# A graph network layer on one core: TensorE subtracts h in the node update, x+h becomes one operation, one row of four is normalised on VectorE, and the edge update is rectified in transposed form

## What is computed

```python
h = jnp.maximum(_layernorm(x, axis=-1), 0.0)
em = jnp.concatenate([h[src], h[dst]], axis=-1)
em = jax.nn.relu(layer_norm(em @ msg_w + msg_b, msg_g, msg_beta)) * edge_weights[:, None]
msgs = jax.ops.segment_sum(em, dst, num_segments=num_nodes)
messages = msgs / (counts + 1e-08) * valid
gate = jax.nn.sigmoid(h @ gate_w + gate_b)
combined = jnp.concatenate([h, messages], axis=-1)
h_new = jax.nn.relu(layer_norm(combined @ upd_w + upd_b, upd_g, upd_beta))
out = x + gate * h_new + (1.0 - gate) * h
```

## Time and profile before

| | |
|---|---|
| three runs, median | 1056.28 us (1055.12 to 1071.27) |
| the profiled execution | 1053.59 us |
| its span, first to last instruction | 1052.1 us |
| DVE, ACT, PE, POOL busy | 79%, 77%, 69%, 58% of the span |
| mean granted TensorE clock | 0.834 |

### The profile page before, as it was taken

One profiled execution on the slowest core, in us unless ns is written; L12 is line 12 of the kernel. 1 busy time (PEld: TensorE's weight loads), 2 busy tenths in 40 slices (PEclk: granted clock), 3 DMA queues, 4 the chain that ended last, 5 costly groups with the idle time before them and its releaser, 6 DMA issues.

```text
span 1052.1 us, 20637 instructions
## 1 busy us (share of the span) xinstructions
PE 729.7 (69%) x4448; PEld 588.4 (56%) x4448; DVE 833.7 (79%) x3740; ACT 811.5 (77%) x3396; POOL 605.7 (58%) x602
## 2 busy tenths in 40 slices
PE   2377686776767677777666547777777778778772
PEld 2256565654545556555545336666665667667661
DVE  7287888886877888778789347999999988888984
ACT  2378787877868788778779258999999977878973
POOL 5555555554545555555555746666666666665557
PEclk9787978887888887788776668999989888988986
DMA  5255655565655666566532211322221121111110
GB/s 147 76 177 175 209 182 190 187 200 179 196 173 192 215 198 199 171 200 206 192 117 68 90 38 62 95 92 83 94 89 54 62 70 54 61 63 58 65 67 34
DMA packets 74548, 133.66 MB, mean 127 GB/s; under 512 B 16134, under 2 KB 18006, under 8 KB 74482
## 3 DMA queue, kind: packets, MB, share of 16 engines
q1 hardware_dynamic: 53868, 97.58, 27.1%
q0 software_dynamic: 18912, 34.84, 11.8%
q10 hardware_dynamic: 1702, 0.53, 0.2%
HBM read 56.01 MB, written 80.81 MB: 130 GB/s over the span
## 4 chain that ended last, share of the span: by engine, by line
ACT 47%; PE 16%; another core or an unknown queue 15%; issue 11%; DVE 7%; POOL 3%; ACTq 1%; DMA 0%; DVEq 0%; POOLq 0%; SPq 0%
ACT hrow L406 14%; ACT junk L413 13%; ACT xload L406 4%; ACT work L444 3%; PE py L1290 3%; POOL out L626 3%; PE pt L1248 3%; ACT lnv L388 2%; PE pm L1313 2%; ACT work L1159 2%; PE pm L1315 2%; ACT rs L393 2%; ACT at L1099 1%; PE py L1254 1%
## 5 line engine op out<-in xcount | busy, mean ns | idle before, releaser
L626 POOL DMA_INDIRECT out<-work,sidx x196 | 202.7, 1034 | 135.3 <-issue 54.2
L413 ACT ACTIVATE junk<-py 128x128 bf16<-128x128 f32 x588 | 155.7, 292 | 74.8 <-remote 64.2
L621 POOL DMA_INDIRECT ring<-in_x,gidx x140 | 141.9, 1013 | 89.7 <-DVE work L465 47.4
L406 ACT ACTIVATE hrow<-xload,nb,rs 128x128 f32<-128x128 f32 x392 | 163.9, 525 | 1.6 <-issue 0.8
L621 POOL DMA_INDIRECT ring<-in_x,src_i x116 | 116.3, 1002 | 68.4 <-issue 31.5
L1290 PE MATMUL py<-w_u,work 128*128 128x129 f32 x784 | 144.9, 341 | 0.0
L1290 PEld LDWEIGHTS py<-w_u,work 128*128 128x128 f32 x784 | 122.7, 238 | 28.2 <-issue 28.2
L413 ACT ACTIVATION_READ_ACCUMULATOR junk<-py 128x1 f32 x588 | 130.7, 223 | 0.0
L1254 PE MATMUL py<-bias,ones 3*128 3x258 bf16 x294 | 66.8, 313 | 77.6 <-ACT work L1099 56.8
L621 POOL DMA_INDIRECT work<-in_x,gidx x56 | 55.8, 996 | 108.9 <-DVE work L465 97.9
L1248 PE MATMUL pm<-ident,work 128*128 128x128 f32 x376 | 72.4, 325 | 63.4 <-ACT work L1104 31.9
(11 more groups left out here) (179 smaller groups left out, 2049.0 us busy)
## 6 DMA issues: line engine op xcount, KB each, us to landing
xload<-in_x SPq DMA_DIRECT2D x98, 256.0 KB
normalised_rows<-hrow SPq DMA_DIRECT2D x98, 256.0 KB
out<-work SPq DMA_DIRECT2D x98, 256.0 KB
running_sums<-acc SPq DMA_DIRECT2D x49, 256.0 KB
staged_target_rows<-work SPq DMA_DIRECT2D x14, 256.0 KB
ring<-staged_target_rows SPq DMA_DIRECT2D x14, 256.0 KB, 2.8
out<-work,sidx POOLq DMA_INDIRECT x196
ring<-in_x,gidx POOLq DMA_INDIRECT x140
```

The costliest lines, as they stand in the source:

```text
L406: last = nc.scalar.activation(dest[:, m, :], rows[:, m, :], ACT.Relu, bias=nb[:, s4, at + m:at + m + 1], scale=rs[:, s4, at + m:at + m + 1])
L413: last = nc.scalar.activation(junk[:, j, k, :], prod[:, k, 0:H], ACT.Square, scale=scale, accum_out=mv[:, slot, at + k, 1:2])
L621: pool.indirect_dma_start(out=dest, out_offset=None, in_=rows, in_offset=bass.IndirectOffsetOnAxis(ap=idx, axis=0), **({} if rows is sums_ ...
L626: pool.indirect_dma_start(out=out, out_offset=bass.IndirectOffsetOnAxis(ap=idx, axis=0), in_=rows, in_offset=None, **if_tail).then_inc(s, 16)
```

## The change

It has four parts, and constants that go with them.

1. **PE subtracts h.** `out = x + h + gate * (rectified - h)`, which is the same sum. In the node stage PE follows the four transposes back with four products of the transposed h and a negative identity into the same accumulation (`back`). Then x + h needs no gate: DVE makes it in one instruction of 512 columns for a group, in place of four of 128 columns, and 1 - gate isn't made there.
2. **One row of four normalised on VectorE.** ACT normalises rows 0 to 2 of a group in the node stage. Row 3 (`LIFTED`) is `(x - mean) * deviation` in one DVE instruction, `lifted_row`, not rectified. The copy out of PSUM now rectifies, and so does the x + h instruction.
3. **The edge update in transposed form.** As the nodes before: DVE scales in one instruction (`scaled`), PE transposes (`turned`, into `pt[0]`), ACT rectifies with gain and shift in one instruction, PE transposes back (`back`, into `pa`), DVE adds `gate * that` in four (`gated_sum`). The final addition comes in the step of the mix, not in the next one.
4. **Constants.** LATE goes from 29 to 26 and UPFRONT from 10 to 13. The special order of the mix in the last steps is dropped.

```diff
-LATE = 29
-UPFRONT = 10
+LATE = 26
+UPFRONT = 13
+LIFTED = G - 1
...
+        def scaled(dve, d, g, slot, at):
+
+            one_mark(d["gamma"], dve, g, nc.vector.tensor_tensor(
+                t_buf[:, g.at % 4], py[:, g.at % 2, :, 0:H],
+                rs[:, slot, at:at + G].unsqueeze(2).to_broadcast([P, G, H]), ALU.mult))
+
+        def gated_sum(dve, d, f, prod):
+
+            d["mix"].after(dve, f)
+            d["back"].after(dve, f)
+            for k in range(G):
+                last = nc.vector.scalar_tensor_tensor(o[:, f.at % 4, k, :], prod[:, k, :], gt[:, f.at % 4, k:k + 1],
+                                                      o[:, f.at % 4, k, :], ALU.mult, ALU.add)
+            one_mark(d["final"], dve, f, last)
...
-                    nd["gain"].after(dve, g)
+                if fin and turned(g):
+                    one_mark(nd["mix"], dve, g, nc.vector.scalar_tensor_tensor(
+                        o[:, g.at % 4], hrow[:, g.at % 4], 0.0, xload[:, g.at % XS], ALU.max, ALU.add))
...
+            def lifted_row(g):
+
+                s4 = (g.at + 1) % 4
+                nd["rstd"].after(dve, g.back(-1))
+                if beyond(g, 4):
+                    dve.wait_ge(s_hst[g.at % 4], g.rounds(16))
+                one_mark(nd["lifted"], dve, g, nc.vector.tensor_scalar(
+                    hrow[:, g.at % 4, LIFTED, :], xload[:, g.at % XS, LIFTED, :], mv[:, s4, LIFTED, 0:1],
+                    rs[:, s4, LIFTED:LIFTED + 1], ALU.subtract, ALU.mult))
...
+                if fin:
+                    ed["rstd"].after(dve, s)
+                    scaled(dve, ed, g, s.at % 4, 3 * G)
...
-                    one_mark(ed["gamma"], dve, g, by_std(t_buf[:, g.at % 4], py[:, g.at % 2], s.at % 4, 3 * G, g_upd))
-                    beta(dve, ed, g, t_buf[:, g.at % 4], be_upd)
...
+                if fin:
+                    gated_sum(dve, ed, g, rows4(pa[:, :]))
...
-                    one_mark(nd["h"], act, g, h_rows(g, hrow[:, g.at % 4], xload[:, g.at % XS], 0))
+                    one_mark(nd["h"], act, g, h_rows(g, hrow[:, g.at % 4], xload[:, g.at % XS, 0:LIFTED], 0))
...
-                    one_mark(nd["back"], pe, g, flip(pm[:, :, :].rearrange("p k h -> p (k h)"), t_buf[:, g.at % 4]))
+                    for k in range(G):
+                        nc.tensor.matmul(pm[:, k, :], t_buf[:, g.at % 4, k, :], ident[:, :], start=k == 0, stop=False,
+                                         is_transpose=True)
+                    for k in range(G):
+                        last = nc.tensor.matmul(pm[:, k, :], ht_dst[:, g.at % 4, k * H:(k + 1) * H], minus_ident[:, :],
+                                                start=False, stop=k == G - 1)
+                    one_mark(nd["back"], pe, g, last)
...
+                    if beyond(g, 3):
+                        ed["final"].after(pe, g.back(3))
                     one_mark(ed["aflip"], pe, g, flip(pa[:, :], acc[:, g.at % 4]))
+                u = s.back(7)
+                if live(u, EG):
+                    ed["gamma"].after(pe, u)
+                    if live(s.back(2), EG):
+                        ed["ht"].after(pe, s.back(2))
+                    one_mark(ed["turned"], pe, u, flip(pt[:, 0, :], t_buf[:, u.at % 4]))
...
+                if live(u, EG):
+                    ed["relu"].after(pe, u)
+                    if live(s.back(5), EG):
+                        ed["at"].after(pe, s.back(5))
+                    elif beyond(u, 1):
+                        ed["final"].after(pe, u.back(1))
+                    one_mark(ed["back"], pe, u, flip(pa[:, :], t_buf[:, u.at % 4]))
...
-            straight_steps(edge_step, EG, 8, 6, tail_step)
+            straight_steps(edge_step, EG, 7, 6, tail_step)
```

More of the change, by code:

```diff
@@ L316, in build @@
             "nb": 1,
-            "gain": 3,
+            "gain": 2,
+            "rest": 1,
             "mix": 1,
@@ L330, in build @@
         }
-        nd = stages("node", {**common, "turned": 1, "back": 1})
+        nd = stages("node", {**common, "turned": 1, "back": 1, "lifted": 1})
         tl = stages("tail", common)
         tl.update(stages("tail", {"msg": 1, "sum": 1, "aflip": 1, "at": 1}))
-        ed = stages("edge", {**common, "stats": 4, "h": 2, "ht": 1, "flip": 2,
+        ed = stages("edge", {**common, "turned": 1, "back": 1, "stats": 4, "h": 2, "ht": 1, "flip": 2,
                              "gamma_m": 1,
                              "gate": 2,
-                             "rest": 1,
                              "msgw": 1,
@@ L458, in gain, with rest @@
                 L.mark(nc.vector.reciprocal(gt[:, b, 0:n], e1[:, b, 0:n]))
[L459 to L461 removed]
+        def rest(dve, d, g, n=G):
+            d["gain"].after(dve, g)
+            b = g.at % 4
+            one_mark(d["rest"], dve, shifted(d, g), nc.vector.tensor_scalar(omg[:, b, 0:n], gt[:, b, 0:n], -1.0, 1.0, ALU.mult,
+                                                                            ALU.add))
         def mix_row(g, k, h, xr, dest):
@@ L530, in node_step @@
                     nd["h"].after(sp, q)
+                    nd["lifted"].after(sp, q)
                     if q.turn is None and q.at == NG - 1:
@@ L742, in node_rows @@
                     L.mark(row_stats(L, s, xload[:, s.at % XS, 2:4], 2))
+                if fin and not turned(g):
+                    rest(dve, nd, g)
                 if between is not None:
@@ L772, in node_sum @@
                 if live(f, NG) and turned(f):
-                    nd["mix"].after(dve, f)
-                    nd["back"].after(dve, f)
-                    for k in range(G):
-                        last = nc.vector.scalar_tensor_tensor(o[:, f.at % 4, k, :], pm[:, k, :], gt[:, f.at % 4, k:k + 1],
-                                                              o[:, f.at % 4, k, :], ALU.mult, ALU.add)
-                    one_mark(nd["final"], dve, f, last)
+                    gated_sum(dve, nd, f, pm)
                 elif live(f, NG):
@@ L1073, in _ @@
                 t_buf[:, TB, 0, :], tail_y[:, 0:H], tail_rs[:, 1:2], g_upd[:, :], ALU.mult, ALU.mult))
-            L.wait()
+            tl["rest"].after(dve, z)
             one_mark(tl["mix"], dve, z, nc.vector.scalar_tensor_tensor(tail_o, tail_h, omg[:, TB, 0:1], tail_x, ALU.mult, ALU.add))
@@ L1119, in node_step, with node_ht @@
                 if live(g, NG):
-                    evacuate(nd, g, ht_dst[:, g.at % 4, :], pt[:, g.at % 2, :], ACT.Copy, "ht", "flip")
+                    node_ht(g)
                 node_h(s)
+            def node_ht(g):
+                if beyond(g, 4) and turned(g.back(4)):
+                    nd["back"].after(act, g.back(4))
+                evacuate(nd, g, ht_dst[:, g.at % 4, :], pt[:, g.at % 2, :], ACT.Relu, "ht", "flip")
             def node_h(s):
@@ L1194, in edge_step @@
                     gates(act, s.back(6), 1)
-                if live(s.back(7), EG):
-                    ed["gate"].after(act, s.back(7))
-                    gated_relu(act, ed, s.back(7))
                 if live(s.back(2), EG):
@@ L1295, in node_step @@
                     nd["h"].after(pe, g)
+                    nd["lifted"].after(pe, g)
                     one_mark(nd["flip"], pe, g, flip(pt[:, g.at % 2, :], hrow[:, g.at % 4]))
```

85 lines of the change are left out of this document (36 added, 49 removed).

## The result

The changed kernel takes 1118.8 us (median of 4 runs, 1111.1 to 1132.4) against 1055.7 us for the kernel before (4 runs, 1051.7 to 1071.3). The ratio is 1.059, with a 95% interval of 1.051 to 1.066: slower by 6%.

What follows compares the result with a forecast made beforehand. PE was taken as the limit: in the node stage where its clock is low or it is late, in the edge stage through a loop with ACT. 1053.6 + 3 (nodes) + 37 (edges) - 4 (end) + 0 (gathers) + 2.7 (median) = 1092 us, range 1078 to 1112.

Steps and rivals of the forecast that it cites:

- a clock that stays at 0.82: Rival: node stage clock doesn't rise, node steps 5.6 us, +35 in place of +3, total 1124 us; chance 0.10.
- the length of the new products: Sign, node stage: the four subtracting products on PE take about 1 us at clock 1.0, double at 0.5.
- the 9.7 to 10: Sign, edge stage: steps of 9.7 to 10 us both before and after the source rows drop out.
- the choice between the two clocks: Node stage: clock 0.92 (lower level 16%) taken, giving +3 us, over 0.82 (36%), giving +35 us.
- with r smaller by the 0.27: Node stage: the upper-level step r, waits included, falls from 5.28 to 5.01 us by DVE's saving.
- the first rival: Node stage: PE's lateness goes with the low clock, node step 4.39 us, -78 us, total 1011; chance 0.21.
- worth nothing while that takes 8.9: Edge stage: relief of DVE (0.73 us) and ACT (about 0.5) gains nothing beside PE's loop of 8.9 us.
- DVE has room by then: Edge stage: the sums' transposes waiting for an earlier step's gated addition cost nothing, DVE needing 7.9 of 9.8 us.
- The 16 us fit in the three steps of 9 us between: Middle: twelve more up-front gathers, 16 us on POOL, cost 0, with 16 as the other end.
- The -4: End: one step of skew less saves 4 us.
- no vanished wait: The vanished wait, chance 0.21: node stage lumps of waiting for PE go with the low clock, -78 us.
- the second rival: Edge stage: PE's lateness is a fixed pause that transposes partly fill, steps fall towards 8.1 us, total 1012; chance 0.11.

Runs made afterwards that it cites:

- plain_after: The changed kernel with every indexed gather of x and h rows replaced by a plain DMA of 128 fixed rows: 840.8 us, ratio 0.810 to the kernel before.
- plain_before: The kernel before with every indexed gather of x and h rows replaced by a plain DMA of 128 fixed rows: 861.1 us, ratio 0.829.
- edge_transposes: The kernel before with eight more transposes per edge step, on data nothing waits for and results nobody reads: 1075.9 us, ratio 1.014.
- edges_only: The kernel before with the transposed edge update alone, node update and constants as before: 1094.9 us, ratio 1.040.
- consts_old: The changed kernel with LATE = 29 and UPFRONT = 10 as before: 1111.9 us, ratio 1.055 to the kernel before.
- fixed_rows: The kernel before with its x and h gathers still indexed but always given the indices 0 to 127: 1063.1 us against 1065.8, ratio 1.002.

## Why the prediction was right and where it was wrong

The direction held, and the loss comes, as forecast, from the work that the change puts on PE. 1118.8 us lies in the stated range, 1010 to 1128, but above the forecast's own, 1078 to 1112: the wide range, which had been stretched to take in most of the rivals, held by luck. The nearest single figure, 1124, was that of a clock that stays at 0.82, and the clock rose. Of the signs, the length of the new products and the clock near 0.9 came; the edge steps, 9.54 and 9.59 us, stayed under the 9.7 to 10. The terms are another matter. The table gives the difference between after and before by stage in us, as predicted, as measured, and between `plain_after` and `plain_before`.

| stage | predicted | measured | without indexed gathers |
|---|---|---|---|
| node steps | +3 | +17.3 | -24.1 (4.05 to 3.78 a step) |
| middle, edge steps 5 to 10 | 0, other end +16 | +14.8 | -1.4 |
| edge steps 10 to 28 | +0.88 a step | +0.54 a step | -0.49 a step (8.63 to 8.14) |
| edge steps 28 to 44 | +1.08 a step | +0.74 a step | +0.19 a step (7.59 to 7.78) |
| end | -4 | +9.6 | +9.1 |

**The node stage.** The working gave DVE's step as 3.79 us, 0.27 less than now. In `plain_before` DVE's node step is 4.05 us long without a wait. In `plain_after` it goes from one gated sum to the next in 203.75 to 207.49 = 3.74, with the lifted row at 205.10 - 204.85 = 0.25, as forecast (at most 0.26):

```profile
203.75 1.11 DVE L506 SCALAR_TENSOR_TENSOR work<-pm,gt,work 128x128 f32<-128x128 f32 x4
...
204.85 0.34 DVE L808 TENSOR_SCALAR hrow<-xload,mv,rs 128x128 f32<-128x128 f32 x1
205.10 0.69 DVE L497 TENSOR_TENSOR work<-py,rs 128x512 f32<-128x512 f32 x1
...
207.49 1.11 DVE L506 SCALAR_TENSOR_TENSOR work<-pm,gt,work 128x128 f32<-128x128 f32 x4
```

So the terms of instructions were right to some hundredths, and the choice between the two clocks was nearly right (0.92 taken, 0.90 measured). With 0.90 the working's own formula gives 5.32 us, an estimate, where 5.47 was measured. The step that failed is "with r smaller by the 0.27": the 1.2 us of lumps in r were taken as a constant beside the work. The working put them down to PE's clock and to a lateness without a cause; `plain_before`, which has none of them, shows that they come with the indexed gathers. As the rows read, they are a time in which PE gets little done, and it has to catch up afterwards. Before, PE had 2.64 us to do in a DVE step of 4.06 and could catch up; now it has 3.62 in 3.74. The lumps grew from 5.27 - 4.05 = 1.22 to 5.47 - 3.78 = 1.69 us a step, and that took back the whole gain of DVE and more. The argument that ruled the first rival out ("leaves it no room to catch up") fits this; it wasn't carried into the sum.

**The edge loop.** The floors were right here too: 8.64 us was read as ACT's own step, and `plain_before` runs at 8.63; 8.1 was forecast for ACT after the change, and `plain_after` runs at 8.14, or 8.2 without step 27, which has no source rows to normalise any more since LATE is 26. The 7.9 for DVE was taken off ACT's 8.64; off DVE's own 174.63 us in 21 steps it would have been 7.6, and nothing hangs on it. What was wrong is "worth nothing while that takes 8.9": in the first stretch ACT was the limit and the gathers added 0.37 us. With the change they add 9.54 - 8.14 = 1.40. The transposes alone don't do that (`edge_transposes`, +0.12). The other suspect is the wait at which the working took nothing, "DVE has room by then", with "if it were late, its whole 1.03 would enter each step" behind it. Waits of the changed kernel, 690 to 840 us:

```profile
PE pt L1271 <- ACT work L1183: 13.5, 11, 2.2
DVE work L506 <- PE pa L1271: 10.9, 6, 2.2
```

And its timeline, DVE and PE in one of these steps:

```profile
814.13 1.13 DVE L506 SCALAR_TENSOR_TENSOR work<-pa,gt,work 128x128 f32<-128x128 f32 x4 [3.31 <-remote]
...
815.40 0.63 PE L1271 MATMUL pa<-ident,acc 128*128 128x128 f32 x4 [1.52 <-DVE work L506]
```

DVE waits 3.3 us for PE's way back, which by its record was done at 810.2, and PE then 1.5 us for DVE to free `pa`: each lateness of PE is now passed on to DVE and returned. No run took this wait away alone, so for the 0.54 us it stays an argument from the rows; that the loss there appears with the edge part and needs the indexed gathers is shown (`edges_only`, `plain_after`). The later stretch is different: from step 31 to 44, where both kernels have dropped the source rows, `plain_before` takes 7.44 us a step and `plain_after` 7.77, so there the transposed update costs 0.33 us by itself.

**The middle.** "The 16 us fit in the three steps of 9 us between" looked at the scatters. The gathers act on PE while they run: `consts_old` gave the 16 us back there. The bound was written down, the value taken was the wrong one.

**The end.** The -4 counted a step of skew less. What counts is the loop within a drained step, where nothing overlaps. In the changed kernel, from one scaling on DVE to the next:

```profile
1080.64 0.69 DVE L497 TENSOR_TENSOR work<-py,rs 128x512 f32<-128x512 f32 x1 [4.19 <-ACT rs L396]
...
1085.30 0.61 PE L1277 MATMUL py<-bias,ones 3*128 3x258 bf16 x2
...
1089.98 0.69 DVE L497 TENSOR_TENSOR work<-py,rs 128x512 f32<-128x512 f32 x1 [3.10 <-ACT rs L396]
```

The scaling, PE's way there, ACT's rectifying and the way back take 1080.64 to 1085.30 = 4.7 us, and PE can't begin the next group's update (L1277) before, since it stands behind them in its queue. The loop takes 9.3 us. Before, the update's own chain ran on DVE and ACT beside PE's products, and a scaling followed the last one after 6.2:

```profile
1026.07 1.12 DVE L476 SCALAR_TENSOR_TENSOR work<-py,rs,g_upd 128x128 f32<-128x128 f32 x4 [1.30 <-ACT rs L393]
...
1032.25 1.13 DVE L476 SCALAR_TENSOR_TENSOR work<-py,rs,g_upd 128x128 f32<-128x128 f32 x4 [1.48 <-ACT rs L393]
```

This one step is 3.2 us longer. The loss at the end is not a sum of such steps, though, because in the kernel before POOL sets the end: from 1020.28 us on it issues one indexed transfer after the other and never waits more than 0.54 us. In the changed kernel its last three groups of scatters wait for DVE's gated sum, 5.35, 3.09 and 1.74 us; the first and the last:

```profile
1086.87 0.98 POOL L649 DMA_INDIRECT out<-work,sidx  x1 [5.35 <-DVE work L506]
...
1101.59 0.98 POOL L649 DMA_INDIRECT out<-work,sidx  x1 [1.74 <-DVE work L506]
```

With and without indexed gathers the end is 9 us longer, and `edges_only` has 6.4 of them. The longest step of the end is the one before those shown, 12.5 us against 7.3, and 12.3 in `edges_only`, `consts_old` and `plain_after`. What makes it so long stays open.

The rivals: the node clock did rise, and the waits stayed all the same (no vanished wait). Half of the second rival was true: the lateness of PE is a pause, and in the first edge stretch idle transposes fit into it nearly for nothing; but the transposed update doesn't profit from it, and that the new waits are why is argued. The predicted sum was +36 us in the spans and +57 came, because the node stage, the middle and the end were each 14 us too low, while the edge loop cost 23 us over 39 steps where 37 had been put down for 40, and the head gave 7 that have no cause in the change.

## What to carry to other kernels

A lump of waiting isn't a constant that can be carried over to the kernel after. Ask what causes it and how much room the engine that is late has to catch up: work moved onto it costs more than its length once that room is gone, and relief of the others is then worth nothing. When an engine is late by no cause that its own rows show, look at what the idle-looking engines issue in the same microseconds; one run with a cheaper form of it told more here than eight variations of the suspected work. And in a stage that drains, count the links between engines in the loop from step to step, not the busy time.

## What the runs showed of the hardware

Indexed gathers on POOL make TensorE late. With 393 of them the kernel before takes 1038.7 us and with plain DMAs of the same size 861.1, 0.45 us for each; the changed kernel (1100 by its ratio) loses 0.66 each. Packets and bytes of POOL's queue are the same, 18912 and 34.84 MB in the page of the kernel before, and in that of `plain_before`:

```profile
q0 software_dynamic: 18912, 34.84, 13.3%
```

Scattered addresses play no part (`fixed_rows`). The Trainium skill, "SBUF — State Buffer", section "SBUF: two separate sides", says that a DMA and a compute operation can't slow each other, and that PE waits on no one at its ports. The plain DMAs agree with it: beside a DMA share of 0.76 DVE's node step in `plain_before` has no wait. The indexed ones cost this kernel 17%, but whether at those ports or elsewhere, and so whether against the page, isn't told by any run here. Nor is it known whether the indexed scatters, which stayed in all kernels, do the same.

TensorE's granted clock in the node stage was 0.82 in the kernel before and 1.00 in `plain_before`, with the same products and transposes, so the low level there came with the indexed gathers. That it was a result of the lateness, and not its cause, isn't shown by itself; for it speaks that in the changed kernel the clock was 0.90 and the lumps were longer, 1.69 us a step to 1.22.
